# A state-space convolution plus an int4 SwiGLU on one core: down pieces one round earlier, a lighter path to the convolution kernel, a new order of the change of phase

## The chip, the core and the metric

The kernel runs on one core of a Trainium2 chip. The core has a matrix engine (TensorE, PE in the profile, with its weight loads as PEld), a vector engine (VectorE, DVE), an activation engine (ScalarE, ACT), a general engine (GpSimd, POOL) and a sequencer that here only issues transfers (SyncE, SP). All run side by side and wait for one another by semaphores. The metric is the device time of one launch in microseconds (us), less is better.

## The reference

The input x has 2048 rows of 1024. Each row is normalised (xn), and the output is x + conv(xn) + ffn(xn).

```
Omega = exp(-2j*pi*arange(L)/L);  g = 2/step*((1-Omega)/(1+Omega));  c = 2/(1+Omega)     # L = 1024
denom = g[:,None] - Lambda[None,:]                      # 64 states
k00,k01,k10,k11 = sums over the states of (Ct*B, Ct*p, q*B, q*p) / denom
K = real(ifft(c*(k00 - k01/(1+k11)*k10)))               # one kernel of length 1024, for all rows
y = causal convolution of every row of xn with K, + D*xn
Wg, Wu, Wd = (int4 words - zero) * scale                # groups of 64; Wg, Wu: 2752 x 1024, Wd: 1024 x 2752
ffn = (silu(xn @ Wg.T) * (xn @ Wu.T)) @ Wd.T
```

## The kernel before

All large products are made in f16 pairs: every f32 operand is split into a high part (made by ScalarE) and the rest (made by GpSimd), and three matmuls stand for one. On top of that the products use a seven-product scheme on 2 x 2 blocks, so that every operand appears in seven forms (A11, A12, S1 to S4, A22 on one side, B11, B21, B22, T1 to T4 on the other); VectorE makes the sums.

**Phase A** makes h = silu(gate) * up. It has 44 units, n = 0 to 43. A unit is seven products of 12 matmuls of 128x512 for one half of the rows (p = 0 or 1) and one tile t of gate and up columns; units 41 and 42 are short ones, for the 64 columns left over. The work on the other engines is written out by hand, beside the unit in which it should run, as one list for each engine: in rounds g = 1 to 9 of four units (4g to 4g+3). Each round beside its units

- loads int4 words (`raw`) and scales (`sz`) as numbered slabs m through two slots (`load_slab`, `slab_gate`, `slab_up`, `slab_down`); slab m may be loaded once slab m-2 has been dequantised (`deq_done`);
- dequantises: ScalarE the high nibbles (`gate_nibble`, `up_nibble`, `down_nibble`, line L893), VectorE the rest (`gate`, `up`, `down_words`: L1477, L1479, L1480);
- splits the weights in seven forms (`w_high` L918, `w_low` L684, `t_sum`), two tiles t in a round;
- moves PE's results out of PSUM (`snap_s1` L960, `snap_s5` L966, `snap_u2` L972, `snap_u3` L978, `silu_first` L984, `silu_second` L990, `c12` L1557, `h_first` L1569, `h_second` L1576), and splits h (`h_s3` L1594, `h_s12` L1603/L1606, `h_s4` L1613, `h_high` L953, `h_low` L703), which is stored to `h_d` (SP, L383);
- makes one piece of the down weights, g - 1: `down_words`, `d_sum`, `d_high` (L939), `d_low` (L693), stored to `w_d` (SP, L389). The last piece, 9, has no round left and is made around units 41 to 43.

Every engine works its list in order, so an instruction that waits holds all that stands behind it. PE's fifth product of a unit needs `snap_u2` of that unit, the third needs `snap_s1`, the seventh `snap_u3`.

The convolution kernel K is made beside units 5 to 24, by `s4_work` on VectorE: one resolvent of 128 x 128 in each of units 8 to 15 (L1660 to L1669), then sums, roots and columns; GpSimd takes the largest |K| over the partitions (L817) for a scale. The forms of xn that the convolution needs are stored to `xc_d` by eight transfers of 1 MB in a row, at unit 2.

**Phase B** makes the down product, with the eleven pieces of `w_d` now held whole: four super-tiles of rows, seven products each, two row blocks s each, of 33 matmuls (L1394). A product needs its `wd` (2.8 MB), its `hr` (0.7 MB for each s) and, from the third on, VectorE's additions to `acc`. Convolution pieces (L1421) stand between them. **The change of phase** is units 41 to 43 and the first product of phase B. There ScalarE issues the first nine pieces of wd 0, 1 and 2 from its own queue (L995), SP issues everything else (L531 for `wd`, L541 for `hr`), and `kshift`, a shifted copy of K, is flipped by PE (L1435).

## Time and profile before

| | us |
|---|---|
| three timed runs, median (lowest, highest) | 1498.66 (1496.56, 1504.98) |
| the profiled execution, its own time | 1495.27 |
| its span | 1493.5 |
| PE busy | 1333.8 (89%) |
| DVE busy | 957.6 (64%) |
| POOL busy | 674.7 (45%) |
| ACT busy | 457.3 (31%) |

The span is what lies between the first and the last recorded instruction. Shares of busy time are means over stages that differ much: phase A ends at about 994 us, phase B begins at about 1005 us. Rows of a timeline carry the start, the length, the line, the shapes, the count of merged instructions, and in square brackets how long the engine stood idle before and what ended that.

### The profile page before, as it was taken

How to read it: one execution, taken by the hardware profiler on the slowest of the kernel's cores; microseconds unless marked ns; L12 is line 12 of the kernel's file. 1: busy time of each engine (PE TensorE's matmuls, PEld its weight loads, DVE VectorE, ACT ScalarE, POOL GpSimd, SP SyncE). 2: the span in 40 equal slices, each digit the busy share in tenths (PEclk: the TensorE clock that was granted, in tenths of full speed). 3: DMA queues.
4: the chain of work that ended last, by engine and by line, in shares of the span. 5: the costliest groups of instructions: out<-in, count | busy, mean ns of one | idle time of the engine just before them, and what ended most of it. 6: DMA issues, size and time to landing. Idle time of an engine off the chain costs nothing. (4 is left out here: it accounts for less than half of the span.)

```text
span 1493.5 us, 17048 instructions
## 1 busy us (share of the span) xinstructions
PE 1333.8 (89%) x6299; PEld 630.9 (42%) x6299; DVE 957.6 (64%) x1057; ACT 457.3 (31%) x801; POOL 674.7 (45%) x484
## 2 busy tenths in 40 slices
PE   1557899988998999989999999449999999999998
PEld 1423444433443444434444444124444444444444
DVE  4744478899999898678898988535233332432341
ACT  3533444434444354444444543221000000000000
POOL 3642466766678688687978786341000000000000
PEclk9978999999999999999999999769999999999999
DMA  5301554343433344344444443779756236335431
GB/s 177 86 29 70 225 166 131 125 133 115 132 124 117 131 134 140 124 139 134 142 134 141 139 137 112 233 247 365 248 185 222 92 109 221 92 110 196 126 101 57
DMA packets 164646, 218.09 MB, mean 146 GB/s; under 512 B 41426, under 2 KB 121940, under 8 KB 162644
## 3 DMA queue, kind: packets, MB, share of 16 engines
q1 hardware_dynamic: 163988, 209.86, 42.8%
q10 hardware_dynamic: 576, 7.14, 1.4%
q8 instruction: 50, 0.82, 0.2%
q14 instruction: 32, 0.26, 0.1%
HBM read 139.64 MB, written 77.34 MB: 145 GB/s over the span
## 5 line engine op out<-in xcount | busy, mean ns | idle before, releaser
L1310 PE MATMUL px<-xo,wo 128*128 128x512 f16 x2016 | 473.9, 389 | 59.1 <-ACT py L960 30.2
L1310 PEld LDWEIGHTS px<-xo,wo 128*128 128x128 f16 x2016 | 200.1, 100 | 308.7 <-issue 26.5
L684 POOL TENSOR_TENSOR wo<-wf,wo 128x512 f16<-128x512 f32 x147 | 236.5, 1619 | 71.9 <-ACT wo L918 71.9
L703 POOL TENSOR_TENSOR hs<-hf,hs 128x512 f16<-128x512 f32 x154 | 210.8, 1375 | 103.2 <-ACT hs L953 96.1
L1394 PE MATMUL px<-wd,hr 128*128 128x512 f16 x1056 | 235.0, 382 | 10.7 <-DMA wd<-w_d 10.7
L1310 PE MATMUL pz<-xo,wo 128*128 128x512 f16 x1008 | 233.6, 382 | 0.0
L1394 PEld LDWEIGHTS px<-wd,hr 128*128 128x128 f16 x1056 | 102.6, 98 | 131.1 <-DMA wd<-w_d 11.2
L1310 PEld LDWEIGHTS pz<-xo,wo 128*128 128x128 f16 x1008 | 99.5, 99 | 120.8 <-issue 4.6
L1925 DVE SCALAR_TENSOR_TENSOR acc<-px,acc 128x512 f32<-128x512 f32 x32 | 22.1, 691 | 155.3 <-PE px L1394 151.3
L953 ACT ACTIVATE hs<-hf 128x512 f16<-128x512 f32 x154 | 94.5, 621 | 80.8 <-DVE hf L1569 48.2
L693 POOL TENSOR_TENSOR ds<-wf,ds 128x512 f16<-128x512 f32 x69 | 104.2, 1511 | 33.1 <-ACT ds_more L939 20.1
L1310 PE MATMUL py<-xo,wo 128*128 128x512 f16 x504 | 117.6, 384 | 0.0
L1479 DVE TENSOR_TENSOR wf<-wf,sz 128x1024 f32<-128x1024 int32 x63 | 113.4, 1800 | 5.7 <-ACT wf L893 3.8
L1394 PE MATMUL pz<-wd,hr 128*128 128x512 f16 x528 | 116.6, 379 | 0.0
L1480 DVE SCALAR_TENSOR_TENSOR wf<-wf,sz 128x1024 f32<-128x1024 f32 x63 | 112.6, 1788 | 2.2
L918 ACT ACTIVATE wo<-wf 128x512 f16<-128x512 f32 x147 | 90.8, 621 | 75.8 <-DVE wf L1480 55.4
L708 POOL TENSOR_TENSOR u<-u,s 128x512 f32<-128x512 f32 x42 | 60.6, 1442 | 56.7 <-ACT u L978 56.2
L1394 PEld LDWEIGHTS pz<-wd,hr 128*128 128x128 f16 x528 | 50.9, 98 | 58.6
L1310 PEld LDWEIGHTS py<-xo,wo 128*128 128x128 f16 x504 | 49.9, 99 | 60.7 <-issue 2.8
L1259 ACT ACTIVATE xc<-ctmp 128x512 f16<-128x512 f32 x8 | 5.0, 629 | 218.1 <-DVE ctmp L1950 218.1
L1477 DVE TENSOR_SCALAR wf<-raw 128x512 int32<-128x512 int32 x63 | 59.2, 939 | 17.4 <-DMA sz<-in_sz_down 12.8
L1264 ACT ACTIVATE us<-ctmp 128x512 f16<-128x512 f32 x16 | 10.1, 629 | 190.2 <-DVE ctmp L1970 190.2
(211 smaller groups left out, 1406.5 us busy)
## 6 DMA issues: line engine op xcount, KB each, us to landing
h_d<-hs SPq DMA_DIRECT2D x154, 256.0 KB, 3.7
hr<-h_d SPq DMA_DIRECT2D x56, 704.0 KB, 4.2
w_d<-ds SPq DMA_DIRECT2D x69, 256.0 KB, 3.9
wd<-w_d SPq DMA_DIRECT2D x4, 2816.0 KB, 12.5
sz<-in_sz_gate SPq DMA_DIRECT2D x21, 512.0 KB
sz<-in_sz_up SPq DMA_DIRECT2D x21, 512.0 KB
sz<-in_sz_down SPq DMA_DIRECT2D x20, 512.0 KB
xc_d<-xo SPq DMA_DIRECT2D x8, 1024.0 KB, 10.5
```

What stands on the lines that cost most here:

```text
L684: pool.tensor_tensor(w_dest(t, j, 1), w_place_of(j), w_dest(t, j, 0), ALU.subtract).then_inc(wlo_done, 1)
L693: pool.tensor_tensor(d_dest(q)[:, 1, :], d_place_of(g, j), d_dest(q)[:, 0, :], ALU.subtract)\
L703: pool.tensor_tensor(hs[:, j, :, 1, :], h_place_of(p, j), hs[:, j, :, 0, :], ALU.subtract)\
L708: pool.tensor_tensor(u3[:, :], u3[:, :], s5[:, :], ALU.add).then_inc(u2_done, 1)
L918: act.activation(w_dest(t, j, 0), w_place_of(j), ACT.Copy).then_inc(whi_done, 1)
L953: act.activation(hs[:, j, :, 0, :], h_place_of(p, j), ACT.Copy)\
L1310: done = pe.matmul(bank[:, :], wo[t % 2][:, j, wp, k * P:(k + 1) * P], xo[p][:, j, xp, k, :], start=(j in (0, 3) and k == 0 and wp == 0 an ...
L1394: done = pe.matmul(bank[:, :], hr[slot][:, k, hp, :], wd[j][:, k, wp, :], start=(OPENS[j] and k == 0 and hp == 0 and wp == 0), stop=(k == ...
L1477: link(dve.tensor_scalar(q[:, 1, :], r, 15, None, ALU.bitwise_and))
L1479: link(dve.tensor_tensor(w, q, sz[:, slot, 1:2, :].broadcast_to((P, 2, 512)), ALU.subtract))
L1480: dve.scalar_tensor_tensor(out=w, in0=w, scalar=WS, in1=sz[:, slot, 0:1, :].broadcast_to((P, 2, 512)), op0=ALU.mult, op1=ALU.mult).then_in ...
L1925: dve.scalar_tensor_tensor(out=part, in0=banks[BANK[j]][s][:, :], scalar=1.0 / (WS * HS), in1=part, op0=ALU.mult, op1=ALU.add).then_inc(ac ...
```

## The change

Six things change.

1. Down piece g is now made in round g, and piece 0 beside units 2 and 3; in the diff every `g - 1` of the down work is `g`, every `g - 2` is `g - 1`. Nothing of piece 9 is left for units 41 to 43. The slabs are renumbered so.
2. The three scalings at the head of a resolvent move from VectorE to ScalarE (`scale_angles`, right after `snap_s5`), and there is a resolvent beside every second unit, 6 to 20, not beside each of 8 to 15. Roots, columns and the scale come five units later.
3. The largest |K| is no longer taken by GpSimd's all-reduce over partitions but by VectorE on 8 rows, a diagonal of these 8 values, and one small matmul by ones; a reduction over 8 columns follows.
4. The eight stores to `xc_d` are spread over rounds 1 to 8.
5. At the change of phase ScalarE issues wd 0 whole and wd 1 but for its last piece, right behind each other, after waiting for the store of the tail piece's first form; later wd 2 and wd 3 together, and wd 4 after unit 43. wd 2 lies in the place of the dequantising buffers. `kshift` has a place of its own, and is loaded before unit 43 is done.
6. In the first super-tile the convolution pieces start two places later and come in pairs at the end.

```diff
 def slab_gate(t):
-    return 2 * t if t <= 2 else 6 * ((t - 1) // 2) + (0 if t % 2 else 3)
+    return 0 if t == 0 else 2 + 6 * ((t - 1) // 2) + (0 if t % 2 else 3)
 def slab_down(g, half):
-    return 65 + half if g == 9 else 6 * (g + 1) + 2 + 3 * half
+    return 6 * g + 4 + 3 * half
...
-        return [] if i < 3 else [10, 11] if i == 13 else [i - 3]
+        return [] if i < 5 else [i - 5] if i < 11 else [2 * i - 16, 2 * i - 15]
...
@@ SP, units 2 and 3
+            load_down(0, 0)
             load_gate(2)
+            sp.wait_ge(xlo_done, 56)
             load_up(2)
-            sp.wait_ge(xlo_done, 56)
-            for p in range(2):
-                for blk, kh, j in ((0, 0, A11), (0, 1, A12), (1, 0, S1), (1, 1, A22)):
-                    store_xc(p, blk, kh, j)
             store_h(0, 0, A11)
             store_h(0, 0, S3)
+            store_w(0, B11)
+            load_down(0, 1)
...
             for j in E_ORDER:
                 store_h(0, 1, j)
+            load_up(3)
+            store_w(0, B22)
...
@@ POOL, end of round 5
-                if g == 5:
-                    pool.wait_ge(kcol_done, 1)
-                    pool.partition_all_reduce(kabs[:, :], kcol[:, :], P, bass.bass_isa.ReduceOp.absmax)\
-                        .then_inc(kabs_done, 1)
...
@@ ACT
+            def scale_angles(n):
+                if n % 2 or not 6 <= n < 6 + 2 * M8:
+                    return
+                m = (n - 6) // 2
+                act.wait_ge(angle_in, 16 * (m + 1))
+                if m == 0:
+                    act.wait_ge(numer_done, 1)
+                else:
+                    act.wait_ge(resolvent_done, m)
+                if m >= 2:
+                    act.wait_ge(cauchy_done, m - 1)
+                re, im, res = s4w[:, 0, :], s4w[:, 1, :], s4w[:, 2 + m % 2, :]
+                co, si = angle[:, 0, :], angle[:, 1, :]
+                act.activation(re, co, ACT.Copy, scale=sc[:, 3:4])
+                act.activation(im, si, ACT.Copy, scale=sc[:, 2:3])
+                act.activation(res, co, ACT.Copy, scale=sc[:, 5:6]).then_inc(scaled_done, 1)
...
-            def load_wd(j):
-                q = split_place(NG - 2, j)
-                act.wait_ge(ds_out[split_slot(q)], 16 * (SPLIT_TURN[q] + 1))
-                act.dma_start(wd[j][:, 0:KC - 2, :, :].rearrange("p k a w -> p (k a w)"),
+            def load_wd(j, k1):
+                for g in (NG - 2, NG - 1, NG)[:2 if k1 < KC else 3]:
+                    q = split_place(g, j)
+                    act.wait_ge(ds_out[split_slot(q)], 16 * (SPLIT_TURN[q] + 1))
+                act.dma_start(wd[j][:, 0:k1, :, :].rearrange("p k a w -> p (k a w)"),
...
@@ ACT, units 41 to 43
             silu_tail(41)
-            load_wd(0)
+            load_wd(0, KC)
+            load_wd(1, KC - 1)
...
-            down_nibble(NG - 1, 0)
             silu_tail(42)
-            load_wd(1)
-            d_high(NG - 1, B11)
...
-            down_nibble(NG - 1, 1)
             snap_s1(43)
...
             silu_first(43)
-            load_wd(2)
+            act.wait_ge(dlo_done, 7 * (NG + 1))
+            load_wd(2, KC)
+            load_wd(3, KC)
+            snap_u3(43)
+            silu_second(43)
+            load_wd(4, KC)
...
@@ DVE, resolvent(m)
-                dve.tensor_scalar(re, co, sc[:, 3:4], None, ALU.mult)
-                dve.tensor_scalar(im, si, sc[:, 2:3], None, ALU.mult)
-                link(dve.tensor_scalar(res, co, sc[:, 5:6], None, ALU.mult))
+                dve.wait_ge(scaled_done, m + 1)
...
@@ DVE, s4_work(n)
-                if 8 <= n < 8 + M8:
-                    resolvent(n - 8)
-                if n == 17:
+                if n % 2 == 0 and 6 <= n < 6 + 2 * M8:
+                    resolvent((n - 6) // 2)
+                if n == 22:
                     cauchy_sums()
                     roots()
```

**ScalarE at units 41 to 43.** L893 is a nibble of down piece 9, L1001 and L1003 are `silu_tail(42)`, L960 is `snap_s1(43)`. Before, from the last forms of the tail on:

```order
L953 ACTIVATE hs<-hf_63 128x4x128 x2
L939 ACTIVATE ds_more<-wf 128x512 x2
L893 ACTIVATE wf<-raw,below 128x512
L1001 ACTIVATE g_61<-px 64x512
L1003 ACTIVATE sil<-py 64x512
L995 DMA wd_80<-w_d 128x9216
L939 ACTIVATE ds<-wf 128x512
L953 ACTIVATE hs<-hf_63 128x4x128 x2
L893 ACTIVATE wf<-raw,below 128x512
L960 ACTIVATE py<-px 128x512
```

Now, from the first load of `wd` on (L917 is `h_high`, L903 `d_high`, L984 and L986 `silu_tail(42)`, L924 `snap_s1(43)`):

```order
L978 DMA wd_79<-w_d 128x11264
L978 DMA wd_80<-w_d 128x10240
L917 ACTIVATE hs<-hf_63 128x4x128
L903 ACTIVATE ds<-wf 128x512
L903 ACTIVATE ds_more<-wf 128x512
L917 ACTIVATE hs<-hf_63 128x4x128 x2
L903 ACTIVATE ds_more<-wf 128x512 x2
L984 ACTIVATE g_61<-px 64x512
L986 ACTIVATE sil<-py 64x512
L917 ACTIVATE hs<-hf_63 128x4x128 x2
L924 ACTIVATE py<-px 128x512
```

Both nibbles are gone from between the tail's forms and `snap_s1(43)`, and two loads of `wd` stand ahead of them.

**SP at the end of phase A.** L389 and L390 store `w_d`, L383 and L384 `h_d`; `hr_86` and `hr_87` are the operands of phase B's first product. Before:

```order
L541 DMA hr_86<-h_d 128x2816
L541 DMA hr_87<-h_d 128x2816
L383 DMA h_d<-hs 128x4x256
L389 DMA w_d<-ds_more 128x1024
L383 DMA h_d<-hs 128x4x256
L578 DMA flip<-in_flip 128x128
L389 DMA w_d<-ds_more 128x1024
L531 DMA wd_79<-w_d 128x2048
```

Now:

```order
L530 DMA hr_86<-h_d 128x2816
L520 DMA wd_80<-w_d 128x1024
L530 DMA hr_87<-h_d 128x2816
L384 DMA h_d<-hs 128x4x256
L390 DMA w_d<-ds 128x1024
L384 DMA h_d<-hs 128x4x256
L568 DMA flip<-in_flip 128x128
L572 DMA kshift<-kpad 128x512 x2
```

The last slices of wd 0 no longer stand here, and `kshift` follows `flip` directly.

**VectorE in unit 2.** L1594 (now L1581) is `h_s3(0, 0)`, L1603 and L1606 (now L1590 and L1593) are `h_s12(0, 0)`. Before:

```order
L1594 TENSOR_TENSOR hf_63<-hf_63 128x512
L1477 TENSOR_SCALAR wf<-raw 128x512
L1479 TENSOR_TENSOR wf<-wf,sz 128x1024
L1480 SCALAR_TENSOR_TENSOR wf<-wf,sz 128x1024
L1603 TENSOR_TENSOR hf_63<-hf_63 128x512
L1606 TENSOR_TENSOR hf_63<-hf_63 128x512
```

Now:

```order
L1581 TENSOR_TENSOR hf_63<-hf_63 128x512
L1464 TENSOR_SCALAR wf<-raw 128x512
L1466 TENSOR_TENSOR wf<-wf,sz 128x1024
L1467 SCALAR_TENSOR_TENSOR wf<-wf,sz 128x1024
L1464 TENSOR_SCALAR wf<-raw 128x512
L1466 TENSOR_TENSOR wf<-wf,sz 128x1024
L1467 SCALAR_TENSOR_TENSOR wf<-wf,sz 128x1024
L1590 TENSOR_TENSOR hf_63<-hf_63 128x512
```

A second group of three, the dequantising of down piece 0, now stands ahead of `h_s12`.

## Rows read from the trace of the kernel before

**Rows 1.** Timeline of PE, 940 to 1160 us: start, length, what, idle before.

```profile
948.91 5.30 PE L1310 MATMUL px<-xo,wo 128*128 128x512 f16 x12 [6.01 <-DVE hf L1586]
...
979.34 4.19 PE L1310 MATMUL px<-xo,wo 128*128 128x512 f16 x12 [22.11 <-ACT py L960]
...
991.13 2.75 PE L1310 MATMUL px<-xo,wo 128*128 128x512 f16 x12
1004.55 16.87 PE L1394 MATMUL px<-wd,hr 128*128 128x512 f16 x66 [10.67 <-DMA wd<-w_d]
...
1025.20 14.41 PE L1394 MATMUL py<-wd,hr 128*128 128x512 f16 x66
```

**Rows 2.** Timeline of ACT, 925 to 1030 us.

```profile
945.76 0.63 ACT L939 ACTIVATE ds<-wf 128x512 f16<-128x512 f32 x1 [13.36 <-DMA w_d<-ds]
...
957.17 0.63 ACT L939 ACTIVATE ds_more<-wf 128x512 f16<-128x512 f32 x1 [1.81 <-DVE wf L1549]
...
978.07 0.72 ACT L893 ACTIVATE wf<-raw,below 128x512 int32<-128x512 uint8 x1 [10.26 <-DMA sz<-in_sz_down]
978.70 0.58 ACT L960 ACTIVATE py<-px 128x512 f32<-128x512 f32 x1
```

**Rows 3.** DMA queues, 990 to 994 us: packets, MB, share of 16 engines.

```profile
q10 hardware_dynamic: 76, 1.40, 100.5%
q1 hardware_dynamic: 32, 0.07, 4.2%
```

**Rows 4.** The page, part 6, DMA issues: KB each, us to landing.

```profile
w_d<-ds SPq DMA_DIRECT2D x69, 256.0 KB, 3.9
```

**Rows 5.** Timeline of PE: fourth product of units 8, 18, 25, 28, 38.

```profile
282.86 2.75 PE L1310 MATMUL py<-xo,wo 128*128 128x512 f16 x12
...
497.77 2.54 PE L1310 MATMUL py<-xo,wo 128*128 128x512 f16 x11
...
626.07 2.75 PE L1310 MATMUL py<-xo,wo 128*128 128x512 f16 x12
...
688.80 2.75 PE L1310 MATMUL py<-xo,wo 128*128 128x512 f16 x12
...
873.23 2.75 PE L1310 MATMUL py<-xo,wo 128*128 128x512 f16 x12
```

**Rows 6.** DVE's instructions on tile s4w (resolvents), 280 to 460 us: busy.

```profile
280.00:460.00 180.00, 54.28 (x80) 0.97 0.39 126
```

**Rows 7.** Groups of DVE by form, 180 to 560 us: busy us, mean ns.

```profile
L1660 DVE TENSOR_SCALAR s4w<-angle,sc 128x128 f32<-128x128 f32 x8 | 9.5, 1191 | 0.0
L1661 DVE TENSOR_SCALAR s4w<-angle,sc 128x128 f32<-128x128 f32 x8 | 7.8, 979 | 0.0
...
L1662 DVE TENSOR_SCALAR s4w<-angle,sc 128x128 f32<-128x128 f32 x8 | 6.8, 850 | 0.0
```

**Rows 8.** Timeline of SP around 717 us: issue of the slab of `up(16)`.

```profile
717.15 0.55 SPq L350 DMA_DIRECT2D sz<-in_sz_up  x1
```

**Rows 9.** Timeline of ACT, 600 to 800 us: its nibble.

```profile
725.81 0.72 ACT L893 ACTIVATE wf<-raw,below 128x512 int32<-128x512 uint8 x1 [5.16 <-DMA sz<-in_sz_up]
```

**Rows 10.** Timeline of POOL, 555 to 612 us: the all-reduce.

```profile
604.21 0.59 POOL L817 PARTITION_ALL_REDUCE kabs<-kcol  x1 [5.96 <-issue]
611.81 1.15 POOL L703 TENSOR_TENSOR hs<-hf,hs 128x512 f16<-128x512 f32 x1 [7.00 <-issue]
```

**Rows 11.** Timeline of ACT in unit 2: `h_high(0, 0, S1)`, ahead of `snap_u2(2)`.

```profile
173.60 0.63 ACT L953 ACTIVATE hs<-hf 128x512 f16<-128x512 f32 x1 [3.24 <-DVE hf L1603]
```

**Rows 12.** Timeline of PE in unit 2: the fifth product.

```profile
174.86 2.75 PE L1310 MATMUL px<-xo,wo 128*128 128x512 f16 x12 [0.47 <-ACT u L972]
```

**Rows 13.** Timeline of DVE, end of unit 3: `h_first(3)`, behind `t_sum(2, T4)`.

```profile
201.39 0.69 DVE L1569 SCALAR_TENSOR_TENSOR hf<-u,g 128x512 f32<-128x512 f32 x1
```

**Rows 14.** Timeline of ACT in unit 4: `up_nibble(3)` and `snap_u2(4)`.

```profile
206.41 0.72 ACT L893 ACTIVATE wf<-raw,below 128x512 int32<-128x512 uint8 x1 [0.47 <-DMA sz<-in_sz_up]
...
210.54 0.60 ACT L972 ACTIVATE u<-px 128x512 f32<-128x512 f32 x1
```

More of the change, by code:

```diff
@@ L230, in s4_plus_int4_swiglu @@
         zrow = small("zrow", [1, P])
-        kabs = small("kabs", [P, M8])
+        kend = small("kend", [M8, 2])
+        kdiag = small("kdiag", [M8, M8])
         kmx = small("kmx", [P, 1])
@@ L1247, in _ @@
             act.wait_ge(kscale_done, 1)
+            for i in range(2, 6):
+                q = max(q for q in SPLIT_TURN if split_slot(q) == i)
+                act.wait_ge(ds_out[i], 16 * (SPLIT_TURN[q] + 1))
             scale = ksc[:, 0:1].bitcast(f32)
@@ L1330, in s4_steps @@
             def s4_steps(n):
-                if 9 <= n < 9 + M8:
-                    m = n - 9
+                if n % 2 and 7 <= n < 7 + 2 * M8:
+                    m = (n - 7) // 2
                     pe.wait_ge(resolvent_done, m + 1)
@@ L1342, in s4_steps @@
                         .then_inc(dft_done, 1)
-                if n == 20:
+                if n == 25:
                     pe.wait_ge(kcol_done, 1)
                     pe.transpose(pv[0][0:M8, 0:P], kcol[:, :], ident[:, :]).then_inc(kt_done, 1)
+                if n == 28:
+                    pe.wait_ge(kmax_done, 1)
+                    pe.matmul(pv[1][:, 0:M8], angle[0:M8, 0, :], kdiag[:, :], start=True, stop=True).then_inc(kall_done, 1)
             for q in range(4):
@@ L1374, in down @@
                 if sp_ == 0:
-                    pe.wait_ge(wd_in[j], 32 if j < 3 else 16)
+                    pe.wait_ge(wd_in[j], 32 if j == 1 else 16)
                 pe.wait_ge(hr_in[slot], 16 * (n // 2 + 1))
@@ L1814, in _ @@
             h_s3(0, 0)
+            down_words(0, 0)
             gate(2)
@@ L1828, in _ @@
             t_sum(2, T4)
+            down_words(0, 1)
+            d_sum(0, T1)
+            d_sum(0, T3)
             h_first(3, 1, 1)
@@ L1849, in _ @@
                 h_s4(g - 1, 1)
-                down_words(g - 1, 0)
+                down_words(g, 0)
                 h_s3(g, 0)
@@ L1868, in _ @@
                 t_sum(2 * g + 2, T4)
-                down_words(g - 1, 1)
+                down_words(g, 1)
                 h_s12(g, 0)
-                d_sum(g - 1, T1)
-                d_sum(g - 1, T3)
+                d_sum(g, T1)
+                d_sum(g, T3)
                 h_s4(g, 0)
@@ L1897, in _ @@
                 d_sum(NG, j)
-            down_words(NG - 1, 0)
             h_s12(NG, 0)
@@ L1901, in _ @@
             h_s4(NG, 0)
-            down_words(NG - 1, 1)
-            for j in T_ORDER:
-                d_sum(NG - 1, j)
             c12(43)
```

260 lines of the change are left out of this document (112 added, 148 removed).

## The prediction

> **What bounds the kernel now.** I read PE's timeline first, for where the matrix engine stands still, since it is busy 89% of the span and phase B is one unbroken run of it. From 1025.20 us on its products follow each other without a gap [rows 1], and the change alters neither their number nor their size, so nothing is won after that point except by getting there sooner. Three stretches before it hold idle time.
>
> The first is the change of phase. Unit 43 starts late by 6.01 us, its third product waits another 22.11 us for `snap_s1(43)`, and phase B waits 10.67 us for `wd` [rows 1]. The first products after a long wait also run at half speed: 5.30 and 4.19 us against 2.75, and 16.87 for 66 matmuls against 14.41 [rows 1].
>
> The second is the stretch of the resolvents. The fourth products of units 8 and 18 stand 214.91 us apart, those of units 28 and 38 stand 184.43 apart, for the same ten units [rows 5]. So the convolution kernel costs PE 30.5 us there, through a VectorE that is out of time. Beside it, GpSimd's all-reduce: from 598.25 (the 5.96 of idle before 604.21) to 611.81 GpSimd does nothing else, 13.6 us [rows 10]. From unit 25 to 28 PE takes 62.73 us [rows 5]; three undisturbed units take 3/10 of 184.43, 55.3.
>
> The third is the fill, before unit 4, where PE hardly waits: 0.47 us at the fifth product of unit 2 [rows 12].
>
> **The change, part by part.**
>
> *Nothing of piece 9 at the end.* `snap_s1(43)` ran at 978.70, behind the nibble of a slab that landed after 10.26 us of waiting [rows 2]. Both nibbles go. What is late next are the tail's own forms, whose last ran at 957.17 [rows 2], then `silu_tail(42)` and two forms of h that wait for VectorE's sums. I count 4 to 5 us for these six short instructions with their sums: `snap_s1(43)` at about 962. From its third product to its end unit 43 took 991.13 + 2.75 - 979.34 = 14.5 us [rows 1], which gives 976.5. The 6.01 us before unit 43 stay: they come from ScalarE's wait of 13.36 us for a store of `w_d` [rows 2], and that store and what stands before it are the same.
>
> *The loads of wd on ScalarE's queue.* wd 0 now waits for the store of the tail's first form, made about when the wait of 13.36 us ends, at 948; a store lands in 3.9 us [rows 4], so the two loads start at 952, 2.88 and 2.62 MB. ScalarE's queue (q10) moved 1.40 MB in 4 us, 350 GB/s, and SP's queue (q1), though transfers were waiting in it, got 4.2% of the engines meanwhile; q10's packets are 18.4 KB in the mean (1.40 MB by 76), q1's 2.2 KB [rows 3]. I take it that what SP issues from 952 on hardly moves until 952 + 5.5/0.35 = 968. Behind that stand seven stores of 0.26 MB up to the tail's form T2, 5.2 us at that rate, and 3 us until the last is seen: 976. Only then does ScalarE get past `load_wd(2)`, and `snap_u3(43)` is behind it. So the seventh product waits some 3 us, and phase A ends at 980, not 994: 14 us.
>
> Then wd 2, 3 and 4 (8.65 MB, 25 us) hold q10 until 1002, just when phase B's first product needs its two `hr` of 0.72 MB on q1. Both ends: if SP's transfers are not held at all, the first product (14.2 us) and the flip (1.6) follow at once and the second product begins at 996 against 1025.20, -29; if they stand still until 1002, the first begins at 1004 and the second at 1020 or, with its slow start, 1023, about 0 to -2. In between, by packets in the proportion of rows 3 (32 to 76) and 5.6 KB against 22.5 KB, the first `hr` gets 37 GB/s and lands in 19 us, at 997; the second stands behind a slice of wd 1 and lands at about 1005; its half takes 7.1 us, then the flip: the second product at 1014. I take **-11**. `acc` and later `hr` are behind this but have 14 us more each, and wd is then three products ahead.
>
> The Trainium skill, in "DMA: Bandwidth & Descriptors", section "Queues, rings and completion order", says that each DMA engine takes turns between the queues it has work for, a whole packet at a time; the trace agrees with turns that favour large packets. By packets in equal number the first `hr` would get a fifth of the bandwidth and land at 988, and the second product would begin at the same 1014, since the second `hr` decides. The page's section "Issuing engines are not separate DMA queues" adds that a second issuing engine saves only issue time, which speaks against a gain from issuing wd there.
>
> *Resolvents.* One costs 54.28/8 = 6.8 us of VectorE [rows 6], of which the three scalings are (9.5 + 7.8 + 6.8)/8 = 3.0 [rows 7]; 3.8 stay. On ScalarE, busy 31%, three instructions of a quarter of the usual width cost less than 1 us in every second unit, after `snap_s5`; VectorE comes to the resolvent later than that, behind its dequantising, so it should not wait. Of the eight, the four beside units 8, 12, 16, 20 stand ahead of `down_words`, and these set when the next `up` slab is loaded: issue at 717.15, nibble at 725.81 after 5.16 us of waiting [rows 8, 9], with `snap_u2` behind the nibble. That chain has no slack, so I count 3.8 us for each of them, 15.2; the other four meet VectorE's idle time before `c12` and count nothing. The roots, some 9 us of small instructions in unit 22, may cost 2. Together 17 in place of 30.5: **-13**. Ends: -25 (only the roots and a little cost) and +1 (the four others cost as much too: 30.4 + 2).
>
> *The maximum.* All-reduce gone: at most 62.73 - 55.3 = 7.4 us [rows 5]. Five tiny VectorE instructions and one small matmul come, under 1 us in a unit with nothing else of this kind. I take **-7**; ends -7.4 and -3, if part of that loss was the slab chain above.
>
> *The fill.* Two things are put on lists that had no slack. In unit 2 `down_words(0, 0)` (about 3.8 us) stands ahead of `h_s12(0, 0)`; ScalarE waits for that in `h_high`, 173.60, with `snap_u2(2)` behind it, on which PE already waits [rows 11, 12]. So +3.8. At the end of unit 3 `down_words(0, 1)` starts where `h_first(3)` stood, 201.39 [rows 13], and takes 3 to 4 us; the slab of `up(3)` may only be loaded after it, and lands 8.7 us later [rows 8, 9], at 214 in place of 206.41; `snap_u2(4)`, four us behind the nibble at 210.54 [rows 14], was needed at 213, when the fourth product ends. +5. The later sums of piece 0 add about 1 in round 1. The eight large stores to `xc_d` leave this stretch, and put 1 MB in each later round, at 350 GB/s 3 us of transfer in 73: nothing either way. I take **+10**; ends 0 (the slabs land sooner without these stores) and +15.
>
> Sum: -11 - 13 - 7 + 10 = -21. From the profiled execution's own 1495.27 this is **1474 us**; that execution was 3.4 us under the median of the timed runs, 1498.66, and 1.3 under their lowest, so a median may lie a little above.
>
> **Rivals.** *A: SP's transfers are not held.* Then the change of phase gives 29 and not 11: 1495.3 - 39 = 1456. For it: the held transfers of rows 3 were small packets, and `hr` has larger ones; against it: 4.2%.
>
> *B: the queue on ScalarE takes back the whole gain at the change of phase* (end 0), with the rest as forecast: -10, 1485. For it: rows 3; against it: there is a gap of about 2 us between the store seen and the next load's first packet in which the first `hr` could get through.
>
> *C: slower.* VectorE and ScalarE now hand each resolvent to one another, in order, from unit 6 on and with the down work of round 1 already beside it. If VectorE has to wait for `scaled_done` about as long as the scalings took (3 us), a resolvent costs its old 6.8 and PE pays it in full, since no chain has slack: 8 x 6.8 = 54 in place of 30.5, +24; with -11 - 7 + 10 that is +16, 1511. It decides from (30.5 + 8)/8 = 4.8 us of PE for each resolvent. Against it: ScalarE's share of 31%, and that before eight resolvents cost 3.8 each.
>
> **How the numbers follow.** Forecast 0.47, A 0.25, B 0.20, C 0.08. A measurement of this kernel can tell 0.5%, 7.5 us, from no change: faster is below 1491, slower above 1506. Forecast and A are faster; of B, with 6 us to either side, 0.14 is faster and 0.06 is not; C is slower but for 0.01. Faster 0.86, same 0.07, slower 0.07. The range for 8 in 10 leaves out C, a third of B and the far end of A: 1452 to 1489.
>
> **What would show it.** In the profile after: `snap_s1(43)` within 5 us of `silu_tail(42)`; ScalarE's first load of wd at about 952 less what was won before; SP's queue under 10% of the engines while q10 runs; PE's wait before its first product of phase B named after `hr`, not `wd`. Fourth products of units 6 and 22 about 16 x 18.4 + 17 us apart. Losses of PE in units 2 and 4 of 4 and 5 us, and no gap of 13 us in GpSimd. It is wrong if phase B starts within 3 us of the end of phase A (rival A), or if `s4w` shows up among the longest waits of VectorE (rival C).

## The result, and the profile after

Four runs of the changed kernel took 1472.47 to 1477.65 us, median 1474.64; four of the kernel before, on the same chip, 1496.56 to 1504.98, median 1499.05. The ratio is 0.9833, 95% interval 0.9815 to 0.9851: 24 us faster. The profiled execution took 1472.47 us with a span of 1470.6, against 1495.27 and 1493.5.

I place the difference by PE's fourth product in each unit, as in [rows 5]. Timeline of PE in the kernel after, at units 8, 24, 25, 28, 38 and 40:

```profile
298.50 2.75 PE L1293 MATMUL py<-xo,wo 128*128 128x512 f16 x12
...
612.09 2.75 PE L1293 MATMUL py<-xo,wo 128*128 128x512 f16 x12
...
630.33 2.75 PE L1293 MATMUL py<-xo,wo 128*128 128x512 f16 x12
...
686.13 2.75 PE L1293 MATMUL py<-xo,wo 128*128 128x512 f16 x12
...
870.14 2.75 PE L1293 MATMUL py<-xo,wo 128*128 128x512 f16 x12
...
908.30 2.75 PE L1293 MATMUL py<-xo,wo 128*128 128x512 f16 x12
```

And in the kernel before, at units 24 and 40:

```profile
607.94 2.75 PE L1310 MATMUL py<-xo,wo 128*128 128x512 f16 x12
...
911.66 2.75 PE L1310 MATMUL py<-xo,wo 128*128 128x512 f16 x12
```

Unit 8 is 15.6 us later than before (the fill), unit 24 only 4.2 later, unit 25 4.3 later, unit 28 2.7 earlier, unit 40 3.4 earlier. The rest lies at the change of phase. Timeline of PE there, to be held against [rows 1]:

```profile
944.15 5.00 PE L1293 MATMUL px<-xo,wo 128*128 128x512 f16 x12 [4.61 <-DVE hf L1573]
...
958.45 4.68 PE L1293 MATMUL px<-xo,wo 128*128 128x512 f16 x12 [6.71 <-ACT py L924]
...
970.73 2.75 PE L1293 MATMUL px<-xo,wo 128*128 128x512 f16 x12
973.32 14.41 PE L1381 MATMUL px<-wd,hr 128*128 128x512 f16 x66
997.65 3.78 PE L1422 MATMUL pv<-kshift,flip 128*128 128x512 f32 x4 [9.92 <-DMA kshift<-kpad]
1001.23 15.45 PE L1381 MATMUL py<-wd,hr 128*128 128x512 f16 x66
```

The 22.11 us of waiting for `snap_s1(43)` have become 6.71, the wait for `wd` is gone, phase B starts at once, and a new wait of 9.92 us stands before the flip, for `kshift`. From the fourth product of unit 40 to phase B's second product it is 92.93 us (1001.23 - 908.30), before 113.54 (1025.20 - 911.66): 20.6 less; that product's slow start (15.45 for 14.41) takes 1.0 back. In sum 15.6 (to unit 8) - 11.5 (to unit 24) + 0.1 - 6.9 (to unit 28) - 0.7 (to unit 40) - 19.6 = -23.0, the difference of the two spans (22.9).

ScalarE there, against [rows 2] (timeline of ACT):

```profile
941.00 0.63 ACT L903 ACTIVATE ds<-wf 128x512 f16<-128x512 f32 x1 [11.95 <-DMA w_d<-ds]
...
957.81 0.58 ACT L924 ACTIVATE py<-px 128x512 f32<-128x512 f32 x1
...
993.50 0.63 ACT L917 ACTIVATE hs<-hf 128x512 f16<-128x512 f32 x1 [11.59 <-DMA h_d<-hs]
```

`snap_s1(43)` ran at 957.81, 20.9 us earlier, and ScalarE's old wait of 10.26 us is gone. And the two queues while ScalarE's `wd` 2 and 3 were on their way, 976 to 980 us, against [rows 3]:

```profile
q10 hardware_dynamic: 92, 1.71, 99.5%
q1 hardware_dynamic: 92, 0.07, 5.2%
```

SP's `flip` (issued at 967.35) and `kshift` (978.10) were among those 5%. The two `hr` had been issued at 963.98 and 965.35, in the gap after `wd` 0 and 1, when SP's queue had 98 to 108%.

The fill: PE, ACT and the SP issue of the slab that unit 5 needs (timelines; the last fence is of windows: PE busy and its granted clock, a share of the full 2.4 GHz).

```profile
179.70 4.92 PE L1293 MATMUL px<-xo,wo 128*128 128x512 f16 x12 [4.77 <-ACT u L936]
...
225.23 4.35 PE L1293 MATMUL px<-xo,wo 128*128 128x512 f16 x12 [5.43 <-ACT u L936]
```

```profile
178.44 0.63 ACT L917 ACTIVATE hs<-hf 128x512 f16<-128x512 f32 x1 [7.31 <-DVE hf L1590]
...
220.80 0.72 ACT L857 ACTIVATE wf<-raw,below 128x512 int32<-128x512 uint8 x1 [6.54 <-DMA sz<-in_sz_up]
```

```profile
212.44 0.55 SPq L351 DMA_DIRECT2D sz<-in_sz_up  x1
```

```profile
179.70:184.50 4.80, 4.80 (x13) 0.54 0.17 55
225.20:229.50 4.30, 4.27 (x13) 0.62 0.50 172
```

Both waits are where the prediction put them: `snap_u2(2)` behind `h_high`, which waits for VectorE's `h_s12` ([rows 11] had 3.24 us, now 7.31), and `snap_u2(4)` behind a nibble whose slab was issued at 212.44. After each, twelve matmuls run near half clock, 4.92 and 4.35 us instead of 2.75. By what a unit loses I mean, here and below, the distance of its fourth product from that of the unit before, less the undisturbed 18.13 us; a wait for `snap_u2(2)` so counts as unit 3's loss. Unit 3 loses 7.09 us and unit 5 7.18 (before 0.64 and 0), unit 7 another 1.75.

VectorE on tile s4w, 280 to 460 and 280 to 590 us (windows, in which it is VectorE's busy time):

```profile
280.00:460.00 180.00, 26.97 (x28) 0.98 0.46 148
280.00:590.00 310.00, 47.46 (x49) 0.98 0.45 148
```

Seven resolvents of seven instructions in 47.46 us are 6.8 us each: the same as the ten instructions before [rows 6]. Seven instructions now take 0.97 us in the mean, ten took 0.68.

### The profile page after: what moved, and what is told of

Its sections match the earlier page's. It is cut to its first block, busy times and chain, and to the rows that moved or that the text cites. A ratio compares the mean times of both kernels' runs of the same rounds, so it can differ in the third digit from the quotient of the medians.

```text
span 1470.6 us, 17062 instructions
## 1 busy us (share of the span) xinstructions
PE 1337.2 (91%) x6301; PEld 632.9 (43%) x6301; DVE 962.1 (65%) x1038; ACT 462.3 (31%) x825; POOL 678.0 (46%) x483
## 4 chain that ended last, share of the span: by engine, by line
PE 39%; DVE 5%; DMA 4%; POOL 4%; SPq 2%; issue 2%; ACT 1%; ACTq 0%; DVEq 0%
PE px L1381 15%; PE pz L1381 8%; PE pv L1408 5%; PE px L1293 4%; PE py L1381 4%; DMA sz<-in_sz_up 2%; PE pz L1293 2%; POOL wo L660 2%; DVE wf L1466 1%; POOL hs L679 1%; DMA kshift<-kpad 1%; DMA w_d<-ds 1%; POOL ds L669 1%; DVE wf L1464 1%; SPq L568 1%
## 5 line engine op out<-in xcount | busy, mean ns | idle before, releaser
L660 POOL TENSOR_TENSOR wo<-wf,wo 128x512 f16<-128x512 f32 x147 | 233.5, 1598 | 85.1 <-ACT wo L882 84.7
L917 ACT ACTIVATE hs<-hf 128x512 f16<-128x512 f32 x154 | 94.4, 621 | 90.7 <-DVE hf L1556 45.1
L669 POOL TENSOR_TENSOR ds<-wf,ds 128x512 f16<-128x512 f32 x73 | 113.0, 1547 | 10.8 <-ACT ds L903 10.8
L1464 DVE TENSOR_SCALAR wf<-raw 128x512 int32<-128x512 int32 x63 | 66.8, 1060 | 3.7 <-DMA sz<-in_sz_up 3.7
## 6 DMA issues: line engine op xcount, KB each, us to landing
xc_d<-xo SPq DMA_DIRECT2D x8, 1024.0 KB, 10.9
```

What stands on the lines that cost most here:

```text
L660: pool.tensor_tensor(w_dest(t, j, 1), w_place_of(j), w_dest(t, j, 0), ALU.subtract).then_inc(wlo_done, 1)
L669: pool.tensor_tensor(d_dest(q)[:, 1, :], d_place_of(g, j), d_dest(q)[:, 0, :], ALU.subtract)\
L917: act.activation(hs[:, j, :, 0, :], h_place_of(p, j), ACT.Copy)\
L1464: link(dve.tensor_scalar(q[:, 1, :], r, 15, None, ALU.bitwise_and))
```

## The experiments

All kernels are edits of the changed kernel. Times are medians; the ratio is to the kernel before, run on the same chip. u8, u24, u40 are PE's fourth product of those units, B2 is the start of phase B's second product, all from the PE timeline of the profiled execution.

```
kernel                       us       ratio [95%]              u8      u24     u40     B2
before                       1499.05  1                        282.86  607.94  911.66  1025.20
after                        1474.64  0.9833 [0.9815,0.9851]   298.50  612.09  908.30  1001.23
all-reduce back              1482.74  0.9898 [0.9858,0.9939]   301.48  616.45  921.24  1015.05
scalings on VectorE          1482.68  0.9898 [0.9858,0.9939]   297.66  620.38  915.96  1009.02
xc stores in a row           1484.46  0.9906 [0.9872,0.9941]   309.40  623.15  919.41  1011.94
h_s12 first                  1472.77  0.9828 [0.9795,0.9861]   295.06  609.04  908.15  1001.65
PE's small matmul later      1473.84  0.9826 [0.9811,0.9842]   299.67  612.68  909.26  1001.52
kshift before hr             1473.58  0.9829 [0.9812,0.9845]   299.74  612.59  909.45  1003.32
nibble late                  1486.75  0.9912 [0.9894,0.9930]   303.67  633.86  925.70  1017.72
small rows of wd (one run)   1481.24                           301.22  616.62  915.73  1011.02
wd behind waits              1476.12  0.9858 [0.9832,0.9884]   296.85  611.03  907.50  1004.93
resolvents behind down       1473.05  0.9840 [0.9809,0.9872]   297.23  607.88  905.44   998.25
most of resolvents left out  1463.43  0.9767 [0.9745,0.9788]   298.73  601.14  897.36   990.27
three edits                  1455.33  0.9738 [0.9713,0.9764]   293.77  604.29  901.55   981.91
```

Unit 8 moves by up to 4.6 us between kernels that don't differ before it (296.85 to 301.48); so only distances from one unit to another are compared below. They scatter too: from unit 8 to 24 the seven kernels that don't differ there (the changed one, all-reduce back, xc stores in a row, h_s12 first, kshift before hr, small rows, wd behind waits) take 312.85 to 315.40 us, and from unit 40 to B2 the kernels with the changed kernel's order of phase take 92.0 to 93.8. Less than that is not told apart. Each profile is of one execution.

### The all-reduce back on GpSimd

```
+ (round 6, GpSimd)  pool.partition_all_reduce(kabs[:, :], kcol[:, :], P, absmax)
- (VectorE, unit 26) max and min of rows, kdiag;  (PE, unit 28) the small matmul
```

> The changed kernel with one part undone: the maximum for the next kernel's scale goes again through GpSimd's all-reduce at the end of round 6. Theory (the maximum is worth its own chain, nothing later takes it back): PE's wait at units 26 and 27 comes back, 7.3 us more than in the changed kernel at the fourth product of unit 27, and the end of the kernel is 7 us later, some 1481.5 us. Rival (the wait at the maximum covered something of ScalarE's or of the transfers at the change of phase, which is given back there): the fourth product of unit 28 is 7 us later but the last first product only 0 to 3 us, 1475 to 1477 us.

GpSimd (timeline of POOL), then PE:

```profile
687.44 0.73 POOL L793 PARTITION_ALL_REDUCE kabs<-kcol  x1 [7.15 <-issue]
695.70 4.49 POOL L680 TENSOR_TENSOR hs<-hf,hs 128x512 f16<-128x512 f32 x4 [7.53 <-issue]
```

```profile
715.56 4.06 PE L1298 MATMUL px<-xo,wo 128*128 128x512 f16 x12 [3.36 <-ACT u L941]
```

From 680.3 to 695.7 GpSimd does nothing else. It stood here at the end of the round's GpSimd list, near unit 28 and not 24, so the wait shows in units 29 to 31 and not 26 and 27, as I had written: from unit 28 to unit 31 PE takes 9.3 us more than in the changed kernel (64.99 against 55.64), and nothing gives it back up to B2. The theory holds; this place costs 9.3 us where the old one cost 7, and the end is 8.1 us later.

### The scalings back on VectorE

```
-  act.activation(re|im|res, ...)          # scale_angles, ScalarE
+  dve.tensor_scalar(re|im|res, ...)       # in resolvent(m), VectorE
```

> The changed kernel with the three scalings of each resolvent put back on VectorE; the schedule (a resolvent beside every second unit) stays. Theory (what was gained up to unit 24 came from the new places of the resolvents, and PE now waits only one unit later, for VectorE's s4w): at each of the 8 resolvents VectorE has 0.3 to 1.2 us of operations more; the four that PE waits for cost 0.4 to 3 us more each, 2 to 12 us in all, best 4: 1478.5 us. Rival (the scalings were what made the resolvents dear, their stay on ScalarE is the gain): units 8 to 24 lose the 11.5 us that they had gained, 1486 us.

From unit 8 to 24 it took 322.72 us against 313.59 in the changed kernel and 325.08 in the one before. So of the 11.5 us won there 9.1 are the scalings': nearer to the rival, which I had given as 11.5. The 2.4 that are left for the new places are no more than the scatter. PE's waits for `s4w` rose from 2.73 to 4.83 us, four times.

### The xc stores in one row

```
+ load_up(2);  for i in range(8): store_xc(i)      # SP, unit 2
- if g <= 8: store_xc(g - 1)                       # SP, each round
```

> The changed kernel with the stores of the convolution's pieces issued in one row beside unit 2, as in the kernel before. Theory: these stores are behind no wait of PE after unit 4, the time is that of the changed kernel, 1473.5 to 1475.5 us. Rival (they hold ScalarE at unit 2 so that the VectorE work before unit 3 is waited for less or more): the 7.1 us loss at unit 3 changes by 2 us or more, to 1470 or 1478 us.

Neither: unit 4 lost 11.80 us instead of 1.52, and unit 8 comes 10.9 later. Timeline of ACT:

```profile
204.66 0.63 ACT L917 ACTIVATE hs<-hf 128x512 f16<-128x512 f32 x1 [10.41 <-DMA h_d<-hs]
```

Eight megabytes fill SP's queue for some 20 us, the small stores of h behind them land late, and ScalarE can't reuse its buffer. In the kernel before the same row stood beside a fill with slack (unit 4 lost 1.81 us); with the down words in units 2 and 3 that slack is used. The spread stores, costed at nothing, are worth 10 us to this change.

### h_s12 ahead of the down words

```
+            h_s12(0, 0)
             down_words(0, 0)
             gate(2)
-            h_s12(0, 0)
```

> The changed kernel with VectorE's h_s12 of the first half unit issued ahead of the down words of piece 0 instead of behind them. Theory (the 7.1 us loss at unit 3 is VectorE's row of down words standing ahead of the work that ScalarE's hs and then PE wait for): the wait before PE's product at unit 3 falls from 4.8 to 0 to 1 us and PE stays at full speed there, the loss at unit 3 is 0 to 1.5 us, and the end 5.5 to 7 us earlier: 1468.5 us. Rival (what is moved from there meets the next wait, the slab behind unit 4's operations): unit 3 is 6 us earlier, unit 5's loss grows by 4 to 6 us, and the end is 0 to 2 us earlier, 1473.5 us.

Between: the wait for `snap_u2(2)` went, but a new one stands five products later, for `snap_s1(3)`. Timelines of PE and ACT:

```profile
190.05 4.45 PE L1293 MATMUL px<-xo,wo 128*128 128x512 f16 x12 [2.61 <-ACT py L924]
```

```profile
188.27 0.72 ACT L857 ACTIVATE wf<-raw,below 128x512 int32<-128x512 uint8 x1 [4.48 <-DMA sz<-in_sz_up]
```

The next slab could only be loaded after the down words, which now run later. Unit 3 loses 4.48 instead of 7.09, and units 3 and 4 together win 3.0. By unit 40 that was gone, but not by this edit: at unit 35 a wait of 1.99 us instead of 1.30 was followed by a start at low clock (4.44 for 2.75), and unit 35 lost 3.84 us, as it did in the kernel with small rows of `wd` (3.94), which has the order of the changed kernel there.

### PE's small matmul one unit later

```
-                if n % 2 and 7 <= n < 7 + 2 * M8:
+                if n % 2 == 0 and 8 <= n < 8 + 2 * M8:
```

> The changed kernel with PE's small matmul of each resolvent one unit later (beside units 8, 10, ... 22 and not 7, 9, ... 21); nothing else moves. Theory (what is left of the resolvents' cost in units 9, 13, 17 and 21, 5.2 to 5.4 us each, is PE standing 2.7 us before that matmul for VectorE's s4w and then restarting at half speed): these four losses fall to under 1 us each, the fourth product of unit 24 is 16 to 21 us earlier, and what is then late next (slabs, down words) gives some of it back: the end 8 to 16 us earlier, best 12: 1462.5 us. Rival (the wait stands for VectorE's work itself, which is late whatever PE asks of it): the losses move to units 10, 14, 18 and 22 with 4 to 5 us each, the end within 3 us of the changed kernel's.

The rival. Units 9, 13, 17, 21 lose 0 to 0.4 us, but 10 and 11 lose 2.03 + 3.11, 14 and 15 1.61 + 3.09, and so on; from unit 8 to 24 it is 313.01 us against 313.59, within the scatter. The wait is now PE's for `snap_u2` (343.48, 2.77 us), behind a nibble that waited 5.10 us for its slab. The wait for `s4w` only showed a VectorE that was late anyway.

### kshift ahead of hr

```
+  flip, kshift loads;  load_hr(0, 0, 0); load_wd(1, KC - 1, KC); load_hr(0, 0, 1)
```

> The changed kernel with the loads of flip and kshift issued on SP's queue ahead of the first two loads of hr and not behind them. Theory (kshift waits because it is issued after wd 2 and 3, at 967 and 978 us, when ScalarE's queue takes the engines; issued before, it lands in the same gap as hr): kshift has landed before the first product of phase B ends, PE's 9.92 us wait goes, and the end is 8 to 10 us earlier unless hr is late by more: 1465.5 us. Rival (what is held is whatever stands last on SP's queue; hr is now in kshift's place): PE waits some 10 to 20 us for hr before the first product or its second half instead, the end is 0 to 8 us later, best +3: 1477.5 us.

```profile
992.65 9.12 PE L1381 MATMUL px<-wd,hr 128*128 128x512 f16 x33 [8.48 <-issue]
1001.60 1.88 PE L1422 MATMUL pv<-kshift,flip 128*128 128x512 f32 x4
```

The rival again (timeline of PE): no wait for kshift, 8.48 us before the first product's second half. The profile names no releaser, but its `hr` was issued at 968.39 and landed 24.2 us later, at 992.6. From u40 to B2 it is 93.87 us, 0.9 longer and no more than the scatter. Here too what stood last on SP's queue when `wd` started was held.

### The up nibbles late

```
-                up_nibble(2 * g + 2)        # ahead of snap_s5(n + 2)
+                up_nibble(2 * g + 2)        # behind silu_first(n + 2); up_nibble(3) likewise
```

> The changed kernel with ScalarE's nibble of the odd up slab behind silu_first and snap_u2 instead of ahead of them in round 1, and those of the even slabs likewise in every round. Theory (at unit 5 PE waits 5.43 us and restarts at half speed because snap_u2 stands behind a nibble whose slab landed at 220.8 us): the wait at unit 5 goes, its loss of 7.2 us falls to 0 to 1.5, and the small waits of 1.1 to 1.5 us in units 31, 35 and 39 go too: the end 7 to 11 us earlier, 1465.5 us. Rival (VectorE's dequantising, which waits for the nibble, is the late one; what is put behind lands later at PE's wo): the loss appears 2 to 4 us smaller at unit 6 or 7 instead, and the later rounds lose 1 to 3 us each: the end 0 to 6 us later, 1477.5 us.

The theory fell and the rival was too small: unit 5 lost 5.87 instead of 7.18, but unit 7 5.33 instead of 1.75, and every round to unit 23 about 4 us more. VectorE's dequantising stood still behind the late nibble (between 300 and 635 us four times, 19.7 us in all). From round 7 on, without resolvents, the late nibble was the better one (units 31, 35, 39 lose 0.08, 0.35, 0.27 instead of 1.25, 1.46, 1.90).

### wd in small rows

```
-  act.dma_start(wd[j][:, 0:11, ...], w_d[j, :, 0:11, :])       # rows of 22.5 KB
+  for k in range(11): act.dma_start(wd[j][:, k], w_d[j, :, k]) # rows of 2 KB, j = 2, 3
```

> The changed kernel with the loads of wd 2 and 3 on ScalarE's queue each in 11 transfers, with rows of 2 KB a partition instead of 22.5 KB; same bytes. Theory (the engines take one row of a transfer from each queue in turn, so that a queue with long rows gets nearly all the bandwidth): between the first load of wd 2 and the end of wd 3 SP's queue has 30 to 60% of the engines whenever it has work, flip and kshift land in 3 to 6 us in place of 10.7 to 12, and PE's wait for kshift falls from 9.9 to 0 to 3 us. Rival (SP's queue is held by something else, its own order or the stores' completion): its share stays at 4 to 6% and PE waits 8 to 12 us as before.

DMA queues, 984 to 988 us:

```profile
q10 hardware_dynamic: 625, 1.13, 73.7%
q1 hardware_dynamic: 626, 0.45, 33.7%
```

Again as many packets of one queue as of the other, and now a third of the engines for SP. The landing was not the 3 to 6 us that I expected: the issues of `flip` and `kshift` took 2.85 and 1.68 us in place of 10.65 and 11.96, but they landed 14.1 and 10.8 to 12.9 us after their issue (27.7 and 13.5 to 16.5 in the changed kernel). PE didn't wait for `kshift`, being later itself. The time went elsewhere: 22 issues took ScalarE 14.45 us, `snap_u3(43)` stood behind them, and PE waited 11.67 us for it. The share by rows is shown, in one run; that the wait for `kshift` goes by it is not, and the edit gains nothing.

### wd 3 and 4 behind waits

```
             load_wd(2, KC)
-            load_wd(3, KC)
             snap_u3(43)
             silu_second(43)
+            act.wait_ge(kshift_in, 32); act.wait_ge(hr_in[2], 16); act.wait_ge(hr_in[3], 16)
+            load_wd(3, KC)
             load_wd(4, KC)
             h_high(NG, 1, A12)
...
```

> The changed kernel with ScalarE's loads of wd 3 and 4 issued only when kshift and the first two hr of the second product have landed (three waits ahead of them); wd 2 stays where it is. Theory (SP's short-rowed transfers are held by the long-rowed ones for as long as these last, so the 9.9 us wait for kshift is the length of wd 3 and 4): flip, kshift and both hr land by about 982, wd 3 and 4 follow in 17 us and are needed only at 1005 and later, PE goes from phase A into the second product without a wait and at full speed: its start 10.5 to 12 us earlier, the end likewise: 1463.5 us. Rival (the bytes must all come before the third and fourth product in any order): PE waits 5 to 10 us for wd 3 or for later hr instead, the end is 0 to 5 us earlier, 1471.5 us.

Timelines of VectorE and PE:

```profile
992.61 1.57 DVE L1566 SCALAR_TENSOR_TENSOR hf<-u,sil 128x512 f32<-128x512 f32 x1 [19.80 <-POOL u L684]
```

```profile
994.32 9.05 PE L1384 MATMUL px<-wd,hr 128*128 128x512 f16 x33 [13.31 <-DVE hf L1566]
```

The transfers did as the theory says, if later than the 982 expected: `kshift` landed 6.3 us after its issue (15.0 in the changed kernel), the waits ended at 987.4, and PE no longer waited for `kshift`. But I had queued ScalarE's pieces of h behind the waits. They started at 988.33 after 13.81 us; GpSimd's sums stand in its list behind the first of them, VectorE's `hf` behind those, and PE's second half waits for `hf` before it may overwrite a bank. B2 came 97.4 us after u40, 4.5 later than in the changed kernel.

### The resolvents behind the down words

```
- (n % 2 == 0 and 6 <= n < 22)
+ RESOLVENTS = (6, 9, 10, 13, 14, 17, 18, 21)      # VectorE, ScalarE; PE one unit later
```

> The changed kernel with the resolvents of units 8, 12, 16 and 20 moved behind VectorE's down words of units 9, 13, 17 and 21 (beside ScalarE's scalings and PE's small matmul one unit later too, and the loads of their angles behind the slab's). Theory A, the prediction's (a resolvent ahead of the down words delays the next up slab, and through its nibble snap_u2 and PE): of the 21.3 us that units 9, 13, 17 and 21 lose, 10 to 17 us go and nothing comes in their place: 1461.5 us. Theory B (over a round VectorE, busy 67 of 74 us, has no room left for the 13 us of resolvents wherever they stand): the losses move to units 10, 11 and so on at the same size, the fourth product of unit 24 within 4 us of the changed kernel's, 1474 us.

Between, much nearer to B: units 9, 13, 17, 21 lose nothing, units 10, 14, 18, 22 lose 2.94, 4.62, 2.95 and 2.93 and units 11 and 19 another 1.82. From unit 8 to 24 it is 310.65 us, 2.9 less, just outside the scatter; the kernel with three edits has the same places and 310.52. The end is not told from the changed kernel's (intervals overlap). Theory A, the prediction's own, is refuted as the main cause.

### Six of seven resolvent instructions left out

```
-                dve.scalar_tensor_tensor(out=im, ...) ... dve.reciprocal(re, re)
                 dve.tensor_tensor(res, res, re, ALU.mult).then_inc(resolvent_done, 1)
```

> The changed kernel with six of VectorE's seven instructions of each resolvent left out (only the last product of each is made); ScalarE's scalings, the loads of the angles and PE's small matmuls stay. Left out is the larger part of the resolvents, so the convolution kernel's values are not the reference's. Theory (what units 8 to 24 take above sixteen undisturbed units, 313.6 - 290.1 = 23.5 us, is VectorE's resolvents, less the 1.5 us in each round that later rounds lose too, and 2 to 3 us for the roots): the fourth products of units 8 and 24 come 298 to 301 us apart, the end 13 to 16 us earlier, 1460 us. Rival (it is the new handshake with ScalarE and the small matmul, or the stores of xc in each round, and not VectorE's time): they stay over 307 us apart, the end at most 6 us earlier, 1470 us.

The fourth products of units 8 and 24 in its PE timeline:

```profile
298.73 2.75 PE L1293 MATMUL py<-xo,wo 128*128 128x512 f16 x12
...
601.14 2.75 PE L1293 MATMUL py<-xo,wo 128*128 128x512 f16 x12
```

302.41 us: 11.2 less, just outside my window and far from the rival's. So six of VectorE's seven instructions in eight resolvents cost PE 11.2 us, 1.4 for each resolvent. In seven of these VectorE was busy for 47.46 us and is now for 9.05, 5.5 less each; but its whole busy time from unit 8 to 24 fell only from 287.07 to 274.50 us, so its other instructions there became longer. Of the 12.3 us above sixteen undisturbed units that stay, unit 23 with the roots loses 5.37, and the rest is about 2 us a round, not far from the 1.3 to 1.9 of later rounds.

### Three edits together

```
+ RESOLVENTS as above;  h_s12(0, 0) ahead of down_words(0, 0)
- load_wd(3, KC);  load_wd(4, KC)                   # before h_high(NG, 1, A12)
  ... h_high(NG, 1, S4)
+ act.wait_ge(kshift_in, 32); act.wait_ge(hr_in[0], 32); act.wait_ge(hr_in[1], 32)
+ load_wd(3, KC);  load_wd(4, KC)
```

> The changed kernel with three edits: ScalarE's loads of wd 3 and 4 behind all of its pieces of h and behind waits for kshift and for the two hr of the third product (in the run before this one the waits stood ahead of the pieces of h, and GpSimd, VectorE and PE were queued behind them); the resolvents of units 8, 12, 16, 20 behind the down words; and VectorE's h_s12 of the first half unit ahead of the down words of piece 0. Theory (the wait for kshift is the length of the long-rowed transfers queued before it landed, and is free to lose): PE goes from phase A into the second product without a wait, which begins 80 to 82 us after the fourth product of unit 40 and not 92.9 us after; the fourth product of unit 40 comes 3 to 7 us earlier than in the changed kernel; the end at 1456 to 1461 us, best 1458.5. Rival (the transfers of this stretch, 5 wd and 6 hr and acc, are bound by their bytes): another wait of 5 to 10 us appears before the second or third product, for hr, acc or wd 3, and the end is 1465 to 1469 us.

```profile
965.95 14.41 PE L1387 MATMUL px<-wd,hr 128*128 128x512 f16 x66
980.20 1.88 PE L1428 MATMUL pv<-kshift,flip 128*128 128x512 f32 x4
981.91 14.41 PE L1387 MATMUL py<-wd,hr 128*128 128x512 f16 x66
996.16 14.41 PE L1387 MATMUL px<-wd,hr 128*128 128x512 f16 x66
```

PE passes the change of phase without a wait after unit 43's third product and at full speed (timeline of PE). `kshift` landed 5.9 us after its issue. u40 to B2 is 80.4 us, 12.6 less than in the changed kernel; u40 is 6.8 earlier, 3.7 of it in units 3 and 4 and 3.1 from unit 8 to 24. The end is a little better than the 1456 to 1461 us expected. The `wd` loads were issued at 991.88 and nothing waited for them. The ratio to the kernel before is 0.9738 [0.9713, 0.9764]; it beats the changed kernel, 0.9833.

## Why the prediction was right, and where its steps were not

The time, 1474 against 1474.64, is right partly by luck, because errors cancel: fill +15.6 for +10, resolvents -11.5 for -13, maximum -6.9 for -7, change of phase -19.6 for -11. A fill 5.6 us dearer and a change of phase 8.6 us cheaper than forecast make most of it.

*The fill.* Places and chains were right (both waits named what was predicted, [rows 11] and the slab). Mis-sized: I counted only the waits, 4 and 5 us; they were 4.77 and 5.43, and the restart at low clock adds 1.6 to 2.2 to each, as [rows 1] already showed for others. Unit 7's 1.75 is the "about 1" of round 1. The "nothing either way" for the stores to `xc_d` was wrong: in a row they cost 10.3 us in unit 4. The end 0 of the fill, "the slabs land sooner without these stores", held the mechanism; its worth was not bounded by what the old fill lost. No run makes the down piece late again, so the cost of its early place is read from the two waits and from the run with `h_s12` first.

*The resolvents.* The sum was near (units 6 and 22 stand 313.8 us apart, forecast 311), two steps were wrong. First, "3.8 stay": 6.8 us stayed, since the remaining instructions became longer. The same operation on the same sizes takes one of two lengths; timeline of DVE, two instructions of one resolvent, in the kernel with the later small matmul:

```profile
349.56 1.13 DVE L1648 TENSOR_TENSOR s4w<-s4w 128x128 f32<-128x128 f32 x1
...
351.88 0.29 DVE L1650 TENSOR_TENSOR s4w<-s4w 128x128 f32<-128x128 f32 x1
```

The long one ran while GpSimd was at work, the short one while it stood idle (timeline of POOL, same kernel):

```profile
349.34 1.20 POOL L679 TENSOR_TENSOR hs<-hf,hs 128x512 f16<-128x512 f32 x1
350.50 1.20 POOL L660 TENSOR_TENSOR wo<-wf,wo 128x512 f16<-128x512 f32 x1
355.62 1.48 POOL L679 TENSOR_TENSOR hs<-hf,hs 128x512 f16<-128x512 f32 x1 [3.92 <-ACT hs L917]
```

So it is throughout. Of the 32 TENSOR_TENSOR of 128x128 in eight resolvents, 4 took over 1 us in the kernel before, 6 with the scalings back on VectorE, and 20 in the changed kernel; each of these overlaps a GpSimd instruction, and none of the 0.29 us ones does. Without the scalings a resolvent runs at another moment, beside GpSimd's work. The Trainium skill, in "SBUF — State Buffer", section "SBUF: two separate sides", says that a VectorE instruction with two inputs in SBUF and a GpSimd instruction that reads SBUF shut each other out for a whole instruction; these counts fit that, though no run here took GpSimd's work away. Taking three instructions out saved VectorE 1.1 us for each resolvent (55.19 against 47.46 us for seven) and PE the same, 9.1/8.

Second, the cause: four resolvents ahead of the down words at 3.8 each, four free. Moving those four won 2.9 us in place of 15. In the mean a resolvent costs PE 1.4 us, and 1.0 with four of them behind the down words ((310.65 - 302.41)/8). I put that down to a VectorE without room, busy 287 of 314 us (window of VectorE in the kernel after, units 8 to 24):

```profile
298.50:612.10 313.60, 287.07 (x282) 0.98 0.45 147
```

That it is room that is short is argued, not shown: the busy share is 91% with most of the resolvents left out (274.50 of 302.41), and the same 282 instructions are busy for 305.33 of 310.65 us with the resolvents behind the down words. Busy time here holds the time in which an instruction stands beside GpSimd's, and is no measure of what VectorE could still take.

*The maximum.* Right, and the run with the all-reduce back confirms that nothing later gives it back.

*The change of phase.* `snap_s1(43)` was forecast for about 962 and ran at 957.81; unit 40 was 3.4 us earlier, so that size was right. The held queue was right in kind: SP got 3 to 5% beside ScalarE's long rows. Three sizes failed. ScalarE's wait ended at 941.00, the form's store was issued at 942.88 and `wd` 0 and 1 at 944.99, 2.1 us later and not 3.9 [rows 4]; the forecast was 952, or 948.6 with unit 40 where it was. They were through at 960, not 968, so `wd` 2 could be issued at 967.28 and PE did not wait at the seventh product: phase A ended 65.2 us after unit 40's fourth product, before 82.2, 17 us and not 14. The two `hr` slipped into the gap from 960 to 968, longer than the 2 us I had named for rival B, so that the second product began 27.8 us after the end of phase A and not 34. And what was held was `flip` and `kshift`, which I had not costed: 9.92 us. "PE's wait before its first product of phase B named after `hr`" was wrong by one transfer. One end was added wrongly: transfers that stand still until 1002 give 1020 for the second product, 5 us less than before and not "0 to -2".

Rival A's test (phase B within 3 us of phase A) came out true while its premise, transfers not held, was false: the test did not tell the two apart. Rival B's loss would by the same turns of the queues have been larger with a shorter gap; no run shows how much. Rival C did not come: no wait of VectorE for `s4w` is in the profile, it was PE that waited for `s4w`, four times 2.7 us, and a resolvent costs PE 1.4 us, not 4.8. No run undoes the change of phase part by part, so how the 19.6 us divide between the missing nibbles and the new order of the loads is not known beyond what the two timelines show: a wait of 22.11 us that became 6.71, one of 10.67 that went, and a new one of 9.92.

The step on packets in proportion to [rows 3] (32 to 76) was wrong and the Trainium skill's turns ("DMA: Bandwidth & Descriptors", section "Queues, rings and completion order") right where both queues have work: 92 to 92 and 625 to 626. Why [rows 3] has 32 beside 76 no run shows. From the mean sizes I take a turn to be one row of a transfer: 18.6 KB for `wd` with rows of 22.5 KB (1.71 MB by 92), 1.8 KB with rows of 2 KB, against under 1 KB on SP's queue.

## What to carry to other kernels

Before long-rowed loads go on a second queue, list what the first queue must still deliver until they end: it gets one short row for each long one (92 packets beside 92, and 5% of the engines). Put the loads behind the landing of that list, and put the wait behind everything that other engines need from the issuing engine. When a wait is taken from an engine that is busy nine tenths of the stretch, compare the distance over the whole stretch, not the wait: four moves here (h_s12, PE's small matmul, kshift, the resolvents) made the named wait vanish and left the time within 3 us. And don't price what is taken from VectorE by its busy time where GpSimd works beside it: three scalings that had been busy for 3.0 us gave back 1.1.

## What the runs showed that I had not expected

- Equal packet counts on both queues, whatever the row: 92:92 at 18.6 KB beside 0.8 KB, 625:626 at 1.8 KB beside 0.7 KB.
- A restart at low clock after short waits: a wait of 1.99 us was followed by 4.44 us for twelve matmuls, one of 1.30 by 2.75, of two waits of 2.24 us one by 4.44 and one by 2.75 (resolvents behind the down words, PE at 411.12 and 333.85), and one of 2.77 us by 2.75 (PE's small matmul later, 343.48). So the length of the wait alone does not tell. Over the two restarts of the fill the granted clock was 0.54 and 0.62.
- 22 transfer issues on ScalarE took 14.45 us while both queues were full; two took 0.81.
- Three instructions fewer on VectorE shortened seven resolvents by 1.1 us each and not by the 3.0 that they had been busy [rows 7]; 20 of the 32 TENSOR_TENSOR of the resolvents ran beside a GpSimd instruction, where 6 had.
- GpSimd's all-reduce of a 128x8 tile holds GpSimd for 15.4 us (680.3 to 695.7), though the record itself is 0.73 us.
